# Routed layer of a fused four-layer kernel: GpSimd's additions held back at two places, unread products in four of TensorE's waits

## The reference, cut to what matters

```python
logits = _gelu(xf @ w_r1 + b_r1) @ w_r2 + b_r2
top_p, top_i = jax.lax.top_k(jax.nn.softmax(logits), 2)      # 2 of 8 experts per token
integrated, v = xf, 0
for _ in range(2):
    ctx = concatenate([integrated, v])
    # a shared expert and the 8 routed ones: hidden = gelu(ctx @ w1 + b1); ctrl = hidden @ w2 + b2
    # alpha, beta, gate = sigmoid, softplus, sigmoid of the three parts of ctrl
    # v_next = alpha * v - beta * (x - mu);  x_next = x + 0.1 * gate * v_next
    # both are summed over the experts with the router's weights
    halt = sigmoid(_gelu(x_next @ w_h1 + b_h1) @ w_h2 + b_h2)
    refined = _gelu(x_next @ w_f1 + b_f1) @ w_f2 + b_f2
    integrated = integrated + halt * refined * integration_weight
    v = v_next
```

## Time and profile before

| | |
|---|---|
| median of 3 runs (lowest, highest) | 791.53 us (787.36, 792.1) |
| the profiled execution | 789.41 us |
| its span | 787.6 us |
| mean granted clock of TensorE | 0.97 |
| TensorE busy | 718.6 us (91%) |
| VectorE busy | 548.5 us (70%) |
| ScalarE busy | 490.2 us (62%) |
| GpSimd busy | 171.4 us (22%) |

### The profile page before, as it was taken

One profiled execution on the slowest core, in us unless ns is written; L12 is line 12 of the kernel. 1 busy time (PEld: TensorE's weight loads), 2 busy tenths in 40 slices (PEclk: granted clock), 3 DMA queues, 4 the chain that ended last, 5 costly groups with the idle time before them and its releaser, 6 DMA issues. The chain is left out here.

```text
span 787.6 us, 15151 instructions
## 1 busy us (share of the span) xinstructions
PE 718.6 (91%) x5098; PEld 403.8 (51%) x5098; DVE 548.5 (70%) x1750; ACT 490.2 (62%) x1343; POOL 171.4 (22%) x163
## 2 busy tenths in 40 slices
PE   6989898899999988998799999988989999899887
PEld 3656664666666322333256666653346666553222
DVE  7699988679997378488858999754065666545533
ACT  3788883578884767698669889416675655422101
POOL 7510321560111177256633000201000000000000
PEclk9899999989999969999899999999999999999889
DMA  5794000274000000000007200000000000000000
GB/s 210 138 294 183 2 2 1 62 143 100 2 2 2 0 1 0 1 0 1 1 1 142 41 2 2 28 1 0 1 1 2 1 1 1 2 0 1 1 1 27
DMA packets 17357, 27.61 MB, mean 35 GB/s; under 512 B 1408, under 2 KB 15360, under 8 KB 16640
## 3 DMA queue, kind: packets, MB, share of 16 engines
q1 hardware_dynamic: 17280, 26.64, 12.7%
HBM read 19.03 MB, written 7.60 MB: 34 GB/s over the span
## 5 line engine op out<-in xcount | busy, mean ns | idle before, releaser
L917 ACT ACTIVATE RING<-RING,NMX 128x256 f32<-128x256 f32 x384 | 191.0, 501 | 37.0 <-DVE NMX L1922 36.9
L1922 DVE CUSTOM_DVE_ANT_0 RING<-bank,ADJM 128x256 f32<-128x256 f32 x384 | 143.9, 414 | 20.6 <-PE bank L1306 18.2
L1353 PE MATMUL bank<-W,RING 128*128 128x128 f32 x768 | 118.5, 280 | 14.1 <-ACT RING L929 12.7
L1353 PEld LDWEIGHTS bank<-W,RING 128*128 128x128 f32 x768 | 88.8, 143 | 35.7 <-ACT RING L917 27.4
L1934 DVE COPY RING<-bank 128x512 f32<-128x512 f32 x144 | 98.6, 686 | 4.1 <-PE bank L1353 3.6
L565 POOL TENSOR_TENSOR small<-small 128x2 f32<-128x2 f32 (+2 forms) x17 | 19.4, 1142 | 254.9 <-DVE small L1783 254.9
L917 ACT ACTIVATION_READ_ACCUMULATOR RING<-RING,NMX 128x1 f32 x384 | 72.9, 190 | 0.0
L831 ACT ACTIVATE RING<-bank,NMX 128x512 f32<-128x512 f32 x64 | 43.3, 683 | 42.4 <-DVE NMX L1851 22.7
L1371 PE MATMUL bank<-RING,ARENA 128*32 128x256 f32 x768 | 62.4, 400 | 0.2
L1511 PE MATMUL bank<-ARENA,W 64*128 64x512 f32 x180 | 60.1, 675 | 2.3 <-DVE ARENA L2140 1.9
L1851 DVE TENSOR_REDUCE NMX<-bank 128x1 f32<-128x512 f32 x64 | 39.4, 678 | 31.9 <-PE bank L1204 31.9
(11 more groups left out here) (272 smaller groups left out, 1322.8 us busy)
## 6 DMA issues: line engine op xcount, KB each, us to landing
scratch<-ARENA SPq DMA_DIRECT2D x18, 192.0 KB, 3.0
ARENA<-scratch SPq DMA_DIRECT2D x6, 576.0 KB, 8.2
W<-in_weights SPq DMA_DIRECT2D x1, 2564.0 KB, 22.2
scratch<-ARENA SPq DMA_DIRECT2D x18, 128.0 KB, 2.7
ARENA<-scratch SPq DMA_DIRECT2D x6, 384.0 KB, 5.8
W<-in_weights SPq DMA_DIRECT2D x2, 1024.0 KB, 13.4
W<-in_weights SPq DMA_DIRECT2D x1, 1905.5 KB, 14.6
scratch<-ARENA SPq DMA_DIRECT2D x18, 64.0 KB, 8.1
```

What stands on the lines that cost most here:

```text
L917: nc.scalar.activation(P_OF(n)[:, q * S:(q + 1) * S], S_OF(n)[:, q, :], ACT.Exp, bias=NMX[:, 2 * t + q:2 * t + q + 1], scale=-1.0, accum_o ...
L1353: mm = nc.tensor.transpose(bk[:, o:o + P], P_OF(n)[:, i:i + P], ident)
L1922: nc.vector.tensor_tensor_reduce(out=S_OF(n)[:, q, :], in0=SBANK(n)[:, q * S:(q + 1) * S], in1=ADJM[:, b, q, :], scale=-1.0, scalar=BIG, o ...
```

## The change

GpSimd waits at two places until VectorE has raised `s_xnext`: ahead of `add1(1, 2)` until `x_next(0)` is done, and ahead of `add1(3, 2)` until `x_next(2)` is done. TensorE gets `rehearse` at four places: 6 products ahead of `weights(0, (2, 3))`, 3 ahead of `weights(0, (6, 7))`, 2 ahead of `hidden(2, ...)` and 4 ahead of `refine(2)`. They are written into the bank that the next product of the six would take, so `ahead` waits for that bank to be emptied, but hands nothing out.

```diff
@@ -443,6 +443,12 @@
                 self.freed.append((emptied, value))
                 return bank[self.banks[(len(self.freed) - 1) % k]]
 
+            def ahead(self, eng):
+
+                k = len(self.banks)
+                eng.wait_ge(*self.freed[-k])
+                return bank[self.banks[len(self.freed) % k]]
+
@@ -705,6 +711,7 @@
             add2(0, 6)
+            pool.wait_ge(s_xnext, 1)
             add1(1, 2)
@@ -737,6 +744,7 @@
             add2(3, 5)
+            pool.wait_ge(s_xnext, 3)
             add1(3, 2)
@@ -1553,10 +1561,12 @@
             gates(0, (0, 1))
+            rehearse(6, r6.ahead(pe))
             weights(0, (2, 3))
             gates(0, (2, 3, 4, 5))
             weights(0, (4, 5))
             betas(0, (4, 5))
+            rehearse(3, r6.ahead(pe))
             weights(0, (6, 7))
@@ -1574,6 +1584,7 @@
             gates(1, (6, 7))
+            rehearse(2, r6.ahead(pe))
             hidden(2, (0, 1, 2, 3, 4))
@@ -1613,6 +1624,7 @@
             alphas(3, (6, 7))
+            rehearse(4, r6.ahead(pe))
             refine(2)
```

## The result

| | changed kernel | kernel before, same comparison |
|---|---|---|
| median us (lowest, highest; executions) | 797.1 (788.67, 806.85; 20) | 789.61 (785.2, 797.83; 20) |
| ratio, with 95% interval | 1.0072 [1.0045, 1.0099] | |
| profiled execution, span, mean clock | 792.74, 790.9, 0.972 | 789.41, 787.6, 0.970 |

Forecast were 789.6 us, a range of 784.5 to 793.5 and a ratio within 1%. The ratio is within 1%, but the time is above the range, and where a gain of 0.9 us was forecast there is a loss.

A forecast was written before the change was run, and what follows sets the result against it. TensorE's waits in the routed layer lose the clock; the layer's end hangs on GpSimd's last addition and `x_next(3)`. -2.3 - 0.8 + 0.2 - 0.3 + 2.3 = -0.9, from 790.5 hence 789.6 us; range 784.5 to 793.5.

The forecast's parts named there:

- Six products, 4.15 us; three more at no cost: First stretch: six end at 278.6, softplus of experts 4 and 5 gain 0.4; three more cost nothing, up to 0.6.
- The rival in which the six are too long: First stretch: VectorE's lateness of 1.2 us goes through, the 2.3 gain is lost; +2.6, 793.1 us, chance 0.13.
- First hold, -0.8: GpSimd's additions held until `x_next(0)` is done: it ends 1.7 us sooner, of which 0.8 gained (0 to 1.7).
- Two products ahead of `hidden(2)`, +0.2: Ahead of `hidden(2)`: products of 1.4 us in a wait of 1.14 cost 0.2 us (0 to 1.4).
- From there to 300 ScalarE is nearly always busy, so 2.3 us is kept: First stretch: full clock brings the tanh of `gates(0, 6)` at 290.35 instead of 292.68; 2.3 us gained (0 to 3.9).
- what was gained arrives there: After `hidden(2)` TensorE is busy almost without a gap to 357, so earlier gains reach that point.
- Second hold, -0.3: `x_next(2)` 3.8 us sooner, but GpSimd's queued additions give it back ahead of `x_next(3)`; 0.3 us gained (0 to 0.5).
- The gap ahead of `refine(3)`, +2.3: TensorE idles 4.9 us ahead of `refine(3)`, the clock falls there; 2.3 us lost (0 to 3.0).
- first, second, fourth and last case: Own forecast (chance 0.45), no clock fall at the end (0.22), second hold pays (0.12), holds do nothing (788.4, 0.08).
- the fourth, 783.8 us: Second hold pays: up to 3.8 us comes through and the gap ahead of `refine(3)` shrinks; -6.7, chance 0.12.
- The rival with the spread: The clock does not fall ahead of `refine(3)`; -3.2, 787.3 us, chance 0.22; mixing with the forecast case would spread runs.

The follow-up runs named there:

- first_products: Kernel before plus only the unread products ahead of `weights(0, (2, 3))` (6) and `weights(0, (6, 7))` (3); 791.38 us, ratio 0.9988.
- after_five: The changed kernel, unaltered, profiled once more; span 785.6 us.
- products: The changed kernel without the two waits of GpSimd, unread products only; 799.68 us, ratio 1.0122.
- fill_refine3: The changed kernel plus six unread products between `halting(2)` and `refine(3)`; 792.06 us, ratio 0.999.
- two_fills: The changed kernel plus two unread products ahead of `betas(1, (2, 3, 4, 5))` and six ahead of `refine(3)`; 787.98 us, ratio 0.9949.
- mid_fill: `two_fills` plus one unread product ahead of `gates(3, (0, 1))`; 787.5 us, ratio 0.9982.
- early_fill: The changed kernel plus two unread products ahead of `betas(1, (2, 3, 4, 5))`, nothing added ahead of `refine(3)`; 790.55 us, ratio 1.0014.
- first_half: `early_fill` without the second hold and without the four products ahead of `refine(2)`; 792.0 us, ratio 1.0025.
- changed_again: The changed kernel, unaltered, measured and profiled a second time against the kernel before; 799.89 us, ratio 1.0041.
- hold2: Kernel before plus only the second wait of GpSimd, until `x_next(2)` is done; 794.86 us, ratio 1.0031.
- changed_third: The changed kernel, unaltered, measured and profiled a third time, four executions; 801.59 us, ratio 1.0138.

## Why the prediction was wrong, point by point

Forecast -0.9 us, measured +7.3 ± 2.5, of which the profiles show 4.3. By them the forecast is off by 2.3 us in `h0-h2` (-2.9 forecast, -0.6 measured), by 1.4 in `h2-r3` (-0.3, +1.1) and by 2.9 behind the layer (nothing, +2.9); the end of the layer is right (+2.3, +2.1).

- *Six products, 4.15 us; three more at no cost.* Right: 4.14 and 2.20 us, and the clock is 1.00 where it was 0.50. The softplus of experts 4 and 5 start at 282.16, 27.2 behind `hidden(0)` against 27.5: 0.3 for the 0.4 of the forecast. The rival in which the six are too long is out.
- *First hold, -0.8.* Right where the clock is kept: `x_next(0)` at 0.69 an operation, and -0.8 in `h0-h2` between `first_products` and `after_five`, the two products ahead of `hidden(2)` included. With the clock low from +40.8 on nothing of it is left.
- *Two products ahead of `hidden(2)`, +0.2.* Not tested alone. 56.4 less the 2.9 of the terms up to here should have given 53.5; with a full clock it is 54.5. Against the mean of before, 57.1, the first half gives -2.6, of which 1.8 (2.3 with the two further profiles) is the clock (forecast 2.3) and 0.8 the hold and these two products: nearly well sized, where it arrives.
- *"From there to 300 ScalarE is nearly always busy, so 2.3 us is kept", and "what was gained arrives there".* This is the step that failed. It took ScalarE alone. TensorE, 2.9 us earlier, then meets `second(1, NE)`, which VectorE has only 1.2 us earlier, and waits 1.59 us where no wait stood before. After it the clock fell in three of five profiles of the changed kernel, at 38.8 to 40.9 us behind `hidden(0)`, and `h0-h2` was 57.2 to 59.0. Where it did not fall it was 54.5. I had priced the clock as a thing lost in one place and gained back; the products moved the place. With the profiles of `products`, `fill_refine3` and `first_products`, which have the same wait, it is five of eight. In the four kernels that fill it (`two_fills`, `mid_fill`, `early_fill`, `first_half`) the clock holds there and `h0-h2` is 54.5 each time.
- *Second hold, -0.3.* Right. The six chained additions took 8.58 us for a forecast 8.36; `alphas(3, 6)` to `x_next(3)` took 12.10 us (378.92 to 391.02) against 12.47 (376.15 to 388.62), and `h2-r3` without a fall at +100 is 77.9 (`changed_again`) for 78.3. The Trainium skill's lock for a whole instruction (SBUF — State Buffer, "Who interferes with whom") would have made this term 0 by way of `pair2(3, 6)`, which was to push GpSimd's row back by 0.7. That one took 0.83 us, and of GpSimd's additions the one that started beside it took 1.53 us instead of 1.26, as three did beside `x_next(2)` before (1.52). That is 0.3, not 0.7, so the term stands.
- *The gap ahead of `refine(3)`, +2.3.* Right: 5.01 us, clock 0.50, +2.1 in the mean, in five profiles of five, and gone with the fill. Waits of 3.04 us (`products`) and 3.87 (`hold2`) at this place lost it as well.
- *Not in the sum: the time at +100 and behind the layer.* These were terms put at nothing without a reason. `h2-r3` is 1.1 and `tr-end` 2.9 longer in the mean of the profiles. Code that the change leaves as it was has the first of these falls too, in three profiles of six, so part of it is chance. That the changed kernel has them more often is what the profiles suggest, and not shown. Against chance alone stand the mean times: filling both gaps took 11.0 us off, where their own stretches show 4.8. Whether a fall in one place makes others likelier, and how, was not settled.
- *The range "holds the first, second, fourth and last case".* It doesn't: the fourth, 783.8 us, lies below 784.5. Nothing hung on it here.

The rival with the spread was told as a gain (787.3, "the clock does not fall before `refine(3)`"). The profiles bear out its reason but not its place. The Trainium skill (TensorE: Matmul & The Clock Gate, "Part 1: The HAM clock gate") says that the look at TensorE's activity runs free of the program; by that the same wait costs the clock in one execution and not in the next. The waits of 1.59 us and 0.91 us do just that, the one of 5.01 us costs it each time, and the 20 executions of the changed kernel spread over 18.2 us. What the forecast lacked is the other half of it: a wait which keeps the clock in a profile may lose it in the next, so one profile of before with a full clock at +102 was no proof that nothing is to be lost there.

## What to carry to other kernels

Where unread products keep the clock in one wait, follow TensorE on to the next engine it meets: it comes there earlier, waits longer, and can lose the clock there, nearer to the path. Before an early result is worth anything, ask what TensorE does between it and the next late one; a gap that moves from ahead of a step with time to spare to ahead of one with none is a loss. Take several executions before a share of a few microseconds is put down to a place: here one profile of the changed kernel said +3.3 us, and 20 executions said +7.

## What was not expected of the hardware

- The same low time costs by where it lies. At a mean clock of 0.965 the kernel before took 789.75 to 795.08 us in some 40 executions, 792.6 in the mean; the changed kernel took 797.3 and 799.0. The 13.7 to 17.1 us of low clock that before has behind `hidden(0)` cost 1.8 us, the 6.8 under `refine(2)` at most 0.4 (`first_half` against `two_fills`); 10.2 us in the attention behind the layer cost 5 to 6 us (395.5 for 389.3 to 390.6).
- Within the changed kernel the time follows the mean clock: 788.67 us at 0.978, 806.85 at 0.955. With the low time estimated as twice the missing share of the span, that is 34.6 and 72.5 us, or 18.2 us more for 38 of low clock.
- The clock fell where TensorE had hardly waited: at 410.6 us in `changed_third`, behind waits of 0.36 and 0.17 us, in a stretch where it was 4.63 of 5 us busy with products of 8 rows and others.
